# An eight-batch, two-layer attention and feed-forward kernel: the residual of six batches added on TensorE, with new openings and last slots

## The reference

```python
x = x + attention0(layernorm(x), ctx)        # softmax over 256 keys, biases on q, k, v, o
x = x + top1_experts(layernorm(x))           # 8 experts, 128 -> 512 -> 128, silu
x = x + attention1(layernorm(x), ctx, pos)   # position bias, softmax with 1 + sum, mask
x = x + spiking_ffn(layernorm(x))            # relu^2, 128 -> 512 -> 128, five threshold steps
```

## Time and profile before

| | us |
|---|---|
| median of 3 runs (370.26 to 373.01) | 370.54 |
| the profiled execution: its own time | 372.42 |
| its span, first to last instruction | 370.5 |
| PE busy / DVE / ACT / POOL in the span | 318.3 / 278.8 / 233.3 / 146.4 |
| mean granted TensorE clock, share of 2.4 GHz | 0.934 |

### The profile page before, as it was taken

The page is one execution under the profiler, slowest core; times in us unless marked ns, Lnnn a source line. Parts: engine busy times, 40 slices in busy tenths (PEclk is TensorE's granted clock), DMA queues, the critical chain, the costliest instruction groups (busy, mean ns, idle before and its releaser), DMA issues.

```text
span 370.5 us, 9195 instructions
## 1 busy us (share of the span) xinstructions
PE 318.3 (86%) x3235; PEld 188.7 (51%) x3235; DVE 278.8 (75%) x693; ACT 233.3 (63%) x524; POOL 146.4 (40%) x227
## 2 busy tenths in 40 slices
PE   5798889889988866899998597899988998898993
PEld 2333444444443465599898342344444443347993
DVE  5699999999993648455672339999999998604676
ACT  2138988998888424345555211698898986845652
POOL 3244635366300312875420578355434310354500
PEclk9899999999998876899999788999999996879999
DMA  4224343452422053255551332121221120000111
GB/s 170 71 75 115 105 109 104 112 144 54 152 65 60 3 140 97 50 140 152 134 132 39 96 95 63 51 54 31 66 66 54 25 54 7 6 2 1 36 37 42
DMA packets 33118, 27.89 MB, mean 75 GB/s; under 512 B 4544, under 2 KB 27968, under 8 KB 33072
## 3 DMA queue, kind: packets, MB, share of 16 engines
q1 hardware_dynamic: 30960, 24.07, 22.9%
q0 software_dynamic: 1248, 2.56, 3.2%
q10 hardware_dynamic: 864, 0.66, 0.6%
HBM read 14.75 MB, written 5.70 MB: 55 GB/s over the span
## 4 chain that ended last, share of the span: by engine, by line
PE 44%; DVE 22%; issue 11%; ACT 11%; DMA 8%; POOL 2%; ACTq 0%; SPq 0%; DVEq 0%; POOLq 0%
DVE nm L809 16%; PE M L403 13%; ACT Pt L664 7%; PE R L349 6%; PE R L1613 4%; DMA Pt<-in_mask 3%; PE M L1631 3%; PE R L1445 3%; PE R L358 3%; PE R L1428 2%; PE M L336 2%; DMA sorted_y<-ysb 2%; PE M L503 1%; ACT Osb L648 1%; PE R L336 1%
## 5 line engine op out<-in xcount | busy, mean ns | idle before, releaser
L809 DVE TENSOR_REDUCE nm<-R 128x2 f32<-128x512 f32 x256 | 161.7, 684 | 8.6 <-PE R L349 7.3
L664 ACT ACTIVATE Pt<-R 128x512 f32<-128x512 f32 x256 | 140.2, 596 | 32.9 <-PE R L358 31.6
L403 PE MATMUL M<-Pt,Vt 128*32 128x256 f32 x1024 | 73.2, 407 | 0.3 <-ACT Pt L664 0.3
L349 PE MATMUL R<-Kt,Qt 32*128 32x256 f16 x512 | 50.9, 277 | 13.2 <-DVE nm L809 11.7
L358 PE MATMUL R<-Qt,Kt 32*128 32x256 f16 x512 | 52.1, 281 | 2.6 <-ACT Pt L664 2.3
L1473 ACT ACTIVATE hf<-R,small_in 128x128 f32<-128x128 f32 x92 | 26.3, 367 | 27.9 <-PE R L1428 27.8
L349 PEld LDWEIGHTS R<-Kt,Qt 32*128 32x128 f16 x512 | 14.6, 93 | 54.8 <-DVE nm L809 44.0
L403 PEld LDWEIGHTS M<-Pt,Vt 128*32 128x32 f32 x1024 | 27.8, 114 | 26.6 <-ACT Pt L664 9.1
L1333 POOL DMA_INDIRECT xt<-normed_x,source x23 | 22.8, 992 | 17.2 <-PE M L1436 11.5
L1428 PE MATMUL R<-x_t,w_t 128*128 128x128 f32 x184 | 25.6, 282 | 0.6 <-DVE x_t L1496 0.5
L336 PE MATMUL M<-ones 128*128 128x512 f16 x65 | 22.3, 458 | 3.9 <-issue 3.9
(11 more groups left out here) (191 smaller groups left out, 526.3 us busy)
## 6 DMA issues: line engine op xcount, KB each, us to landing
w_ff<-in_w SPq DMA_DIRECT2D x8, 512.0 KB, 4.0
Pt<-in_mask SPq DMA_DIRECT2D x8, 256.0 KB
Kt<-k_rows SPq DMA_DIRECT2D x8, 256.0 KB, 2.8
Qt<-q_hi SPq DMA_DIRECT2D x30, 64.0 KB, 1.9
k_rows<-Pt SPq DMA_DIRECT2D x24, 64.0 KB
sorted_y<-ysb SPq DMA_DIRECT2D x23, 64.0 KB
Qt<-q_const SPq DMA_DIRECT2D x16, 64.0 KB, 3.5
Qt<-q_lo SPq DMA_DIRECT2D x16, 64.0 KB, 1.9
```

Source lines behind the costliest of these rows:

```text
L349: mm = pe.matmul(row_bank(b, h)[:, q, :], Qt[b % NBUF][rows_of(h), h // HG, q * P:(q + 1) * P], Kt[b % NBUF][rows_of(h), h // HG, :], star ...
L403: mm = pe.matmul(o_bank(b)[KB * i:KB * i + KB, tile * S:(tile + 1) * S], Vflat[par][:, at:at + KB], Pt[g][:, i, k * S:(k + 1) * S], start= ...
L664: act.activation(Pt[i // 2][:, 2 * j + hh, :], key_bank(b, 2 * i + hh).rearrange("p k n -> p (k n)"), ACT.Exp, scale=1.0 / SC).then_inc(ly ...
L809: v.tensor_reduce(nm[par][:, h // 8, :, h % HG, h // HG % 2], row_bank(b, h), AX.X, ALU.max, negate=True)\
```

## The change

For batches 0 to 5 of both layers the product L503 is preceded, in the same PSUM group, by eye x X, so that M[1] holds the new X. ACT copies it back behind exp(4); DVE's addition is gone there. POOL adds the output bias ahead of the norm in slots 0 and later. In the last slots (s = 7, and s = 8 of layer 1) o_copy, the last m_copy and the aT copy go to DVE, batch 7's key banks become a ring of five (p2 waits for head 2i-4), and PE's order at the end of s = 7 is changed. In the opening of layer 0, SP issues both key DMAs and ACT the q_const DMA; DVE makes q_lo ahead of the norm; the clearing of the other two key tiles goes from DVE to POOL; fillers go from 12 to 8 there and from 16 to 10 in layer 1. The keys and values of batches 3 to 6 are made behind the branch. The feed-forward's statistics are taken in five parts where there were three, and its slot -1 is called inside s = 8.

```diff
+        LAST_RING = (4, 5, 3, 1, 2)
         def key_bank(b, n):
-            return R[:, RING + (H * b + n) % RING, :, :]
+            return R[:, LAST_RING[n % len(LAST_RING)] if b == B - 1 else RING + (H * b + n) % RING, :, :]
+        def added_on_tensor(b):
+            return b < B - 2
+        def on_vector(ly, b):
+            return b == B - 2 or b == B - 1 and ly["position"]
...
@@ PE, scores: p2's wait @@
-                    if b > 0 or i >= 1:
+                    if b == B - 1:
+                        pe.wait_ge(ly["exp_done"], H * b + (2 * i - 3 if i >= 2 else i - 1))
+                        if i == 1:
+                            pe.wait_ge(ly["max_done"], H * B)
+                    elif b > 0 or i >= 1:
                         pe.wait_ge(ly["exp_done"], H * b + 2 * i - 1)
@@ PE, slot_fn @@
+                if ffn and s == B:
+                    ffn_start(ffn, -1)
                 if s == -2 and ly["position"]:
-                    keep_running(pe, M[1][:, :], 16)
+                    keep_running(pe, M[1][:, :], 10)
...
-                    keep_running(pe, spare, 12)
+                    keep_running(pe, spare, 8)
...
                     pe.wait_ge(ly["aT_copied"], b)
+                    add = added_on_tensor(b - 1)
+                    if add and ly["bias"]:
+                        pe.wait_ge(ly["x_biased"], b)
                     for q in range(QT):
+                        if add:
+                            pe.matmul(M[1][:, q * D:(q + 1) * D], eye[:, :], X[:, (b - 1) * QT + q, :], start=True, stop=False)
                         mm = pe.matmul(M[1][:, q * D:(q + 1) * D], aT[:, q * P:(q + 1) * P], W["o", ly["index"]][:, :],
-                                       start=True, stop=True)
+                                       start=not add, stop=True)
...
+                    if s == B - 1:
+                        pair(6)
                     pv(b, par, 0)
-                pair(6)
+                if s != B - 1:
+                    pair(6)
+                else:
+                    pair(7)
                 if cur:
                     pv(b, par, 1)
-                if ffn and s == B - 1:
+                if s != B - 1:
+                    pair(7)
+                elif ffn:
                     ffn_start(ffn, -3)
-                pair(7)
@@ ACT @@
-            if b == -2:
-                act.wait_ge(ly["k_hi"], 1)
-                act.wait_ge(inited, INIT_TILES)
-                for block in (0, 2):
-                    act.dma_start(Kt[0][block:P:4, :, :], k_hi[:, :]).then_inc(ly["k_rep"], 16)
...
-                if old:
+                if old and not on_vector(ly, b - 1):
                     o_copy(b - 1, 1 - par)
                 if ffn and s == B:
                     ffn_start(ffn, -2)
-                if cur:
+                    ffn_start(ffn, -1)
+                if cur and s != B - 1:
                     m_copy(b, 1)
...
+                if s == -2 and ly["bias"]:
+                    act.wait_ge(inited, INIT_Q)
+                    act.dma_start(Qt[0][3:P:4, :, :], q_const[:, :, :]).then_inc(ly["q_tile"], 16)
...
                 exp(4)
+                if old and added_on_tensor(b - 1):
+                    act.wait_ge(ly["op_done"], b)
+                    act.activation(X[:, (b - 1) * QT:b * QT, :].rearrange("p q d -> p (q d)"), M[1][:, 0:S], ACT.Copy) \
+                       .then_inc(ly["x_added"], 1)
@@ DVE @@
-            for i in range(1, NBUF):
-                v.memset(Kt[i][:, :, :], 0.0).then_inc(inited, 1)
-            v.wait_ge(inited, INIT_SECOND)
-            for i in range(1, NBUF):
-                v.tensor_scalar(Kt[i][:, :, :], Kt[i][:, :, :], rows[:, 0:1], None, ALU.add).then_inc(inited, 1)
...
+                if old and on_vector(ly, b - 1):
+                    o_copy(b - 1, 1 - par)
+                if s == B - 1:
+                    last_m_copy()
                 r(0)
...
-                if old:
+                if old and not added_on_tensor(b - 1):
+                    if b == B - 1:
+                        v.wait_ge(ly["x_added"], B - 2)
                     v.wait_ge(ly["op_done"], b)
@@ POOL @@
+        def clear_keys(pool):
+            for i in range(1, NBUF):
+                pool.memset(Kt[i][:, :, :], 0.0).then_inc(cleared, 1)
+            pool.wait_ge(loaded, 16 * N_LOADS)
+            pool.wait_ge(cleared, 4 + NBUF - 1)
+            for i in range(1, NBUF):
+                pool.tensor_scalar(Kt[i][:, :, :], Kt[i][:, :, :], rows[:, 0:1], 0.0, ALU.add, ALU.add).then_inc(cleared, 1)
...
+                if s >= 0 and nxt and ly["bias"]:
+                    pool.wait_ge(ly["ob_made"], 1)
+                    pool.tensor_tensor(X[:, (b + 1) * QT:(b + 2) * QT, :], X[:, (b + 1) * QT:(b + 2) * QT, :],
+                                       ob[:, :].unsqueeze(1).to_broadcast([P, QT, D]), ALU.add).then_inc(ly["x_biased"], 1)
                 if 0 <= s <= B - 4:
                     norm_root(pool, b + 3, ly["xvar"], ly["xrstd"])
@@ SP @@
                 if s == -1 and ly["bias"]:
-                    sp.wait_ge(inited, N_INIT)
+                    sp.wait_ge(cleared, 4 + 2 * (NBUF - 1))
@@ feed-forward @@
-        FFN_PARTS = (0, B - 2, B - 1, B)
+        FFN_PARTS = (0, 2, B - 2, B - 1, B)
...
                     if s == -1:
+                        pe.wait_ge(ly[1]["o_copied"], B)
+                    if s == 0:
                         pe.wait_ge(ly[1]["x_added"], B)
@@ PE, between the experts and layer 1 @@
-            ahead_on_tensor(pe, KV_EARLY, KV_LAST)
             pe.wait_ge(mk["any"], 1)
...
             with pe.Else():
+                ahead_on_tensor(pe, KV_EARLY, KV_LAST)
                 attention_on_tensor(pe, ly[1], False, ffn)
```

More of the change, by code:

```diff
@@ L733, in slot_fn @@
                 exp(6)
+                exp(7)
                 if ffn and s == B - 1:
                     ffn_start(ffn, -3)
[L736 removed]
             slots_loop(act, slot_fn)
@@ L790, in first_keys_on_vector @@
             v.tensor_scalar(Kt[0][:, :, :], Kt[0][:, :, :], rows[:, 0:1], None, ALU.add).then_inc(inited, 1)
+            v.tensor_scalar(q_const[:, :, :], q_const[:, :, :], rows[0:KB, 1:2], None, ALU.add).then_inc(inited, 1)
             v.tensor_scalar(vb[:, :], ones32[:, :], qkb[:, 2:3], None, ALU.mult).then_inc(inited, 1)
-            v.tensor_scalar(q_const[:, :, :], q_const[:, :, :], rows[0:KB, 1:2], None, ALU.add).then_inc(inited, 1)
         def other_tiles_on_vector(v):
@@ L832, in o_norm, with o_copy, last_m_copy, a_copy @@
                                 ALU.mult).then_inc(ly["ot_norm"], 1)
+            def o_copy(b, par):
+                v.wait_ge(ly["pv_done"], NG * (b + 1))
+                if b >= 2:
+                    v.wait_ge(ly["ot_done"], b - 1)
+                v.tensor_scalar(Osb[par][:, :, :].rearrange("p t n -> p (t n)"), o_bank(b)[:, :],
+                                rows[:, 2:3] if ly["position"] else 0.0, None, ALU.add).then_inc(ly["o_copied"], 1)
+            def last_m_copy():
+                v.wait_ge(ly["mT_done"], 2 * B)
+                v.wait_ge(ly["m_rows"], 16 * (2 * B - 2))
+                v.tensor_copy(mT[1][:, :], M16[0][0:2 * KB, 0:S]).then_inc(ly["mT_copied"], 1)
+            def a_copy(b):
+                v.wait_ge(ly["aT_done"], b + 1)
+                v.wait_ge(ly["op_done"], b)
+                v.tensor_copy(aT[:, :], M[1][:, 0:S]).then_inc(ly["aT_copied"], 1)
             def applied(b):
@@ L864, in slot_fn @@
                         first_tiles_on_vector(v)
+                    if s == -2 and ly["bias"]:
+                        v.wait_ge(ly["q_hi"], 1)
+                        v.wait_ge(ly["q_copied"], 1)
+                        v.tensor_tensor(q_lo[par][:, :], qf[:, :], q_hi[par][:, :], ALU.subtract).then_inc(ly["q_lo"], 1)
                     if s < -1:
@@ L900, in slot_fn @@
                     o_norm(b - 1)
+                if old and on_vector(ly, b - 1):
+                    a_copy(b - 1)
+                if ffn and s == B - 1:
+                    ffn_stats(v, 1)
                 r(2, (1,))
@@ L998, in slot_fn @@
                     norm_apply_on_gpsimd(pool, ly, b + 3, nxt, 1 - par)
-                if nxt and ly["bias"]:
+                if s < 0 and nxt and ly["bias"]:
                     pool.wait_ge(ly["ob_made"], 1)
@@ L1072, in slot_fn @@
                     tile = Qt[(b + 2) % NBUF]
-                    sp.dma_start(tile[3:P:4, :, :], q_const[:, :, :]).then_inc(ly["q_tile"], 16)
+                    if s != -2:
+                        sp.dma_start(tile[3:P:4, :, :], q_const[:, :, :]).then_inc(ly["q_tile"], 16)
                     if ly["position"] and s >= 1:
@@ L1084, in slot_fn @@
                     sp.dma_start(tile[2:P:4, :, :], q_lo[par][:, :]).then_inc(ly["q_tile"], 16)
+                    if s == -2 and ly["position"]:
+                        for j in range(KV_EARLY + 2, KV_LAST):
+                            ahead_high_on_sync(sp, j)
```

(6 more changed lines are left out.)

33 lines of the change are left out of this document (14 added, 19 removed).

## The result

The changed kernel took 378.81 us in the median of four runs (373.97 to 380.60), the kernel before 371.53 beside it: ratio 1.0131, interval 1.0071 to 1.0191. It is slower by 1.3 to 2%, where 368.8 was forecast, in a range from 364.0 to 373.8. The profiled execution took 379.38 us (span 377.4, before 370.5), at a mean granted clock of 0.917 (0.934).

What follows compares the result with a forecast made beforehand. No engine alone was taken to bound an attention slot: a relay in layer 0, PE's longer leg in layer 1. Terms +3.3 + 2.2 - 1.6 - 0.6 - 3.3 - 1.3 - 0.4 = -1.7 gave 368.8 us, range 364.0 to 373.8.

Steps and rivals of the forecast that it cites:

- (a): Steady slots: identity product and ACT's copy add 0.55 us a slot; +3.3 in layer 1, +2.2 in layer 0.
- (b): Opening of layer 0: first reduction gains 2.5 us at best, POOL's clearing takes some back; -1.6, bounds -2.6 and 0.
- (c): Opening of layer 1: products behind PE's stand at the branch, six fillers fewer; transposes 0.6 us earlier, -0.6.
- (d): Last slots: exponentials undisturbed and clock kept up, -3.3 in layer 1 and -1.3 in layer 0; feed-forward -0.4.
- the +2 bound: Opening of layer 1: if the stand lasts until 209.94 all the same, products end near 216.5, costing +2 us.
- The 1.1 us: Layer 0's steady slots: gain taken for moving POOL's bias addition away from DVE's small multiplication, out of 1.55 us.
- the 1.55 us: Layer 0's steady slots: excess of five slots over the 12.07 us round trip, 0.31 a slot, read as POOL's collision.
- Layer 0's 1.3: Last slot of layer 0: x_added of batch 6, and with it the router, comes 1.3 us earlier.
- 1: Rival: steady slots pay nothing, since DVE, the fullest engine, loses 0.4 us a slot; 363.3, half of it 366; chance 0.22.
- 2: Rival: product and copy in series at 0.85 us in all twelve steady slots; +3.6, 372.4; chance 0.14.
- 3: Rival: the clock falls in the last slots as before; +2.9 and +0.8 on the forecast, 372.5; chance 0.12.
- 4: Rival: the openings don't gain, SP behind POOL's clearing, products behind the branch; +1.6 and +2.6, 373.0; chance 0.10.

Runs made afterwards that it cites:

- e4: Changed kernel with the key tiles cleared by DVE and the products of batches 3 to 6 ahead of the branch, both as before: 371.84 us, ratio to before 0.9988.
- e6: e4 with all residuals also added by DVE, without the identity products and ACT's copies of X: 369.41 us, ratio to before 0.9868.
- e12: Kernel before, with only the clearing of the second and third key tiles moved to POOL: 378.19 us, ratio to before 1.0101.
- e1: Changed kernel with the clearing of the second and third key tiles given back to DVE: 375.23 us, against 374.19 for the kernel before beside it.
- e10: e6 with the attention's last two slots also as before the change: 372.50 us, ratio to before 0.9974.
- e11: Kernel before, unedited, for a second profiled execution: 370.01 us in one run.
- e9: Changed kernel with one addition in place of two in each of POOL's tensor_scalar passes on the key tiles: 380.31 us in one run.
- e13: e6 with more fillers in layer 0's opening, twelve in slot -2 and more in slot -1: 367.52 us, ratio to before 0.9838.
- e3: Changed kernel with all residuals added by DVE as before, and no copy of X by ACT: 376.68 us, ratio to before 1.0069.

## Why the prediction was wrong

Sign and range failed; 1.7 us of gain were forecast, 7 of loss came. The sum again, with what each term measured:

| term | forecast | measured |
|---|---|---|
| (a) steady slots | +5.5 | +2.4 (e4 to e6), by the trace +2.8 in ten of the twelve slots |
| (b) opening of layer 0 | -1.6 | e12 +3.8 to 5.5, e1 3.6 to 5.3 |
| (c) opening of layer 1 | -0.6 | +3.4 (e1 to e4), by the trace +2.8 |
| (d) last slots, join | -5.0 | -3.0 (e10), -4.3 to -4.8 against before beside it |

With (b) at 3.8 to 5.5 and (d) at -3.0 these make +6.6 to +8.3, with (d) at -4.3 some 1 to 2 us less; the loss was 6.6 and 7.3 by the medians, so the parts account for it within their own uncertainty. What else is in (b), the earlier first reduction, gave nothing that can be told from no change: e10, which has it, POOL's move and the feed-forward's new parts, is at 0.9974, interval 0.9937 to 1.0010.

The two profiled spans differ by 6.9 us, and not all of that is in these parts: +4.4 up to exp(0) of slot 1 in layer 0, +0.7 and +1.9 in the five periods of each layer, +1.7 from s = 7 of layer 0 to layer 1, -4.7 behind slot 6 of layer 1, and +2.9 in one slot, s = 6 of layer 0 (11.90 and 14.80 us from exp(0) to exp(0)). That slot follows the clock in all sixteen profiles: 11.8 to 12.3 without a low stretch in it, 13.1 to 13.8 with one of 3.4 us, 14.1 to 14.8 with 6.8. The profile of before had none, but e11 and e12 had 3.4; the mean of those three is 12.75, of the other thirteen 13.55. Whether the change makes the fall there more frequent stays open.

The step that failed is in (b): "POOL's clearing is four passes over 1024 columns; by its memset of 1152 at 1.05 us about 4 us, an estimate, so it ends near 15.5". The memsets took 1.0 each, as said, but the other two passes read and compute, 3.70 us each; the end was 20.58, not 15.5, and "up to 1 us later" became 6.1. The wait for `cleared` and the k product behind it were named; the price was taken from the wrong operation. The profile of before had the right one: POOL's own tensor_scalar on 128x128 (xn, L771) takes 0.80 us, 24 times over. Eight times the columns at that rate is 6.4 us a pass, against 1.0 by the memset: bounds of 1.0 and 6.4, of which I took the low end, and the range should have reached several us further up. The Trainium skill (GPSIMD Engine Reference, "4.1 Engine selection") has one-input work on GpSimd at roughly line rate; the passes of 3.70 us here, 2.84 with one addition (e9), beside 0.44 on DVE, don't bear that out.

A second step of (b) was left out: what PE does while the opening is shorter. "The first reduction gains 2.5 us at best" was about right for the first reduction (2.4 to 3.3 against the first profile of before, 1.5 to 2.4 against e11), and silent on slot -1, where the pairs now wait for DVE. PE's idle time there brought the low clock and ate the gain, until e13 filled it.

(c) looked at PE alone. The products at the lower clock behind the stand came as forecast; the +2 bound was near. The stand was taken to keep its length, and grew by 1.4 us. What was not asked is who waits for the products: the L618 remainder stands ahead of the norm on DVE, and the norm stands ahead of the gathers on POOL. The edit was costed as a move on one engine's queue, and its price lay in the queues of two others.

(a) had the mechanism and not the size: 0.25 a slot in layer 1 and 0.44 in layer 0, not 0.55. The product takes 0.32 us, where 0.47 was taken, and pair 5 and the turn cover ACT's copy; in layer 1 the lower end given, 0.3, was right. The 1.1 us that were taken off for POOL's collision had no ground: the collision is gone (the small multiplication, L817 before and L843 now, takes 0.18 to 0.22 us in slots 1 to 6), and the five periods are as long as before. The reading behind it was wrong. Of the 1.55 us over five round trips, 1.2 stands in e11 too, whose five periods take 61.56 us although the multiplication takes 0.18 in each of them.

(d) was right in the slot itself (8.84 for "near 9") and too high as a sum. In layer 1, from exp(0) of s = 6 to the end, the three profiles of before, e11 and e12 have 64.8 to 67.0 us (mean 66.0), the twelve with new ones 60.8 to 64.4 (mean 62.6): -3.4, against 3.7 forecast for slots and join. e10's own profile, with the old slots, has 63.0, because its clock stayed up.

Layer 0's 1.3 is there and is lost again: from exp(0) of s = 7 to layer 1 it is 121.8 us in the six profiles with the new slots and the products ahead, 121.5 in the kernels before, 123.15 in e10. The end of batch 7 in layer 0, timeline of ACT and DVE and one row of busy time (columns as in rows 1), first in the changed kernel, where exp(0) of s = 7 is at 119.91, then before, where it is at 111.91:

```profile
129.91 0.60 ACT L671 ACTIVATE Osb<-M 128x512 f32<-128x512 f32 x1 [1.22 <-PE M L417]
132.48 1.62 DVE L1194 TENSOR_SCALAR Pt<-X,mv_all,rstd_all 128x128 f32<-128x128 f32 x6 [3.20 <-POOL rstd_all L1212]
134.41 0.43 DVE L856 TENSOR_TENSOR attn<-M,rc 128x256 f32<-128x256 f32 x1
139.00 0.42 DVE L968 TENSOR_TENSOR X<-M,X 128x256 f32<-128x256 f32 x1 [2.63 <-PE M L525]
133.00:137.00 4.00, 3.76 (x18) 3.29 (x19) 3.34 (x13) 1.53 (x4) 0.00 (x0) 0.61 0.00 0
```

```profile
126.14 0.60 ACT L648 ACTIVATE Osb<-M 128x512 f32<-128x512 f32 x1 [1.19 <-PE M L403]
126.06 1.63 DVE L1122 TENSOR_SCALAR Pt<-X,mv_all,rstd_all 128x128 f32<-128x128 f32 x6 [3.20 <-POOL rstd_all L1140]
127.99 0.43 DVE L830 TENSOR_TENSOR attn<-M,rc 128x256 f32<-128x256 f32 x1
130.97 0.42 DVE L913 TENSOR_TENSOR X<-M,X 128x256 f32<-128x256 f32 x1 [1.02 <-PE M L503]
126.00:131.00 5.00, 4.03 (x37) 3.57 (x34) 3.89 (x15) 2.30 (x6) 0.00 (x0) 1.00 0.02 5
```

Counted from exp(0), the copy of batch 7's result comes 4.2 us earlier (10.0 and 14.2). Its division stands on DVE behind the router's normalisation, which waits for POOL's root, and comes 1.6 us earlier (14.5 and 16.1). Batch 7's X comes at 19.1 both times, since PE's products up to it now run at the lower clock. In the twelve profiles with new slots this low stretch begins 13.2 to 16.3 us behind exp(0), in the four with old ones 21.0 to 23.0.

Of the rivals, 1 came half true for another reason, 2 did not come, nor did 3 in the changed kernel's last slots, and 4 (373.0) had the right places and less than half the size: +4.2 on the forecast, where (b) and (c) came out 9 to 11 us above it. What the prediction left open about a memset, e12 shows: q_lo took 0.42 us at 12.52, wholly beside POOL's memset that ended at 13.03, as long as without one.

## What to carry to other kernels

Price a moved operation by a row of the same engine and the same kind of operation, scaled by its size, and never by a cheaper cousin: a pass that reads cost POOL 2.8 to 3.7 times its memset and 6 to 8 times DVE's pass. When work moves past a wait, walk every engine that waits for its result and list what stands behind it in that engine's queue; the loss of layer 1's opening was two queues away from PE. Read a small gain off several profiles: e3's beside the first one of before has POOL's new place at -0.7 us, five beside three have it at nothing. And an opening that gets shorter leaves PE idle between its pairs: look whether the granted clock holds there before the gain is booked, and put fillers where PE waits for another compute engine.

## What the runs showed of the hardware

- POOL's tensor_scalar on 128x1024 f16 with a scalar out of a tile: 3.70 us with two additions, 2.84 with one; DVE 0.44 with one; POOL's memset of the same tile 1.0.
- Two casts of 128x128 on DVE that take 0.25 and 0.21 us in e4 took 1.10 and 1.04 beside POOL's memsets in the changed kernel: an instruction that reads nothing from SBUF held them up too. q_lo, with two inputs from SBUF, was not held up by one (0.42 us in e12).
- In each of the eight profiles with the product one slot of layer 1 is 0.3 to 0.9 us longer, and a DMA of maximum rows lands 3.2 to 3.8 us after its issue near it, where 1.85 is usual (3.69 for the one at 274.95 in the changed kernel). DMAs as late are in the other eight profiles too, but only three of those have such a slot.
- PE's stand at the branch is 3.4 to 4.2 us in ten profiles with 3.6 us of products ahead of it, and 4.5 to 6.2 in six with them behind it.
- One execution of this kernel differs from another by up to 2.5%, in step with the mean granted clock (correlation -0.8 over the 74 runs of the kernel before).
